# A graph network on one NeuronCore: long VectorE operations cut in pieces, other last groups, a shorter carry, a bias added by TensorE

## What is computed

```python
h = x @ W1 + b1
m = relu(concat([h[dst], h[src] - h[dst]]) @ W2 + b2)
m = relu(m @ W3 + b3)
x = layernorm(x + relu(segment_max(m, dst)))        # edge network

def gat(x, W, a_s, a_d, bias):                      # src, dst with loops added
    h = x @ W
    e = leaky_relu((h @ a_s)[src] + (h @ a_d)[dst])
    ex = exp(e - segment_max(e, dst)[dst])
    alpha = ex / segment_sum(ex, dst)[dst]
    return segment_sum(alpha[:, None] * h[src], dst) + bias

y = relu(gat(relu(gat(x, C1, ...)), C2, ...))
x = layernorm(x + y)
```

## Time and profile before

| | us |
|---|---|
| median of 3 runs | 5880.39 |
| lowest, highest | 5874.37, 5883.29 |
| the profiled execution's own time | 5872.45 |
| its span | 5871.2 |
| PE, DVE, ACT, POOL busy | 4931.6, 4098.0, 2658.7, 4399.4 |

### The profile page before, as it was taken

How to read it: one execution, slowest core, us unless ns; L and a number is a source line. 1 busy time by engine, 2 the same in 40 slices (tenths; PEclk the granted TensorE clock), 3 DMA queues, 4 the chain that set the end, 5 groups by cost and what they waited for, 6 DMA issues and landing times.

```text
span 5871.2 us, 119756 instructions
## 1 busy us (share of the span) xinstructions
PE 4931.6 (84%) x29429; PEld 3060.9 (52%) x29429; DVE 4098.0 (70%) x10676; ACT 2658.7 (45%) x8225; POOL 4399.4 (75%) x4585
## 2 busy tenths in 40 slices
PE   3688888888888729999999999943999999999991
PEld 2566666666666525555555555522555555555550
DVE  4344454444445448888888888864888888888886
ACT  2233333333333235555555555533555555555554
POOL 7777777777777677777777777767777777777775
PEclk6899999999999959999999999976999999999995
DMA  6677777777777724444444444432444444444442
GB/s 157 187 219 217 215 223 216 217 219 217 220 217 216 202 59 120 123 124 122 124 125 124 125 124 124 125 92 63 124 123 124 124 125 124 124 124 121 125 125 83
DMA packets 808269, 874.81 MB, mean 149 GB/s; under 512 B 133438, under 2 KB 635185, under 8 KB 807818
## 3 DMA queue, kind: packets, MB, share of 16 engines
q0 software_dynamic: 146016, 295.63, 19.7%
q1 hardware_dynamic: 390298, 361.70, 18.8%
q10 hardware_dynamic: 271504, 213.69, 13.9%
HBM read 536.74 MB, written 331.81 MB: 148 GB/s over the span
## 4 chain that ended last, share of the span: by engine, by line
POOL 51%; issue 21%; DVE 9%; PE 7%; DMA 6%; ACT 3%; DVEq 0%; POOLq 0%; SPq 0%; ACTq 0%
POOL ring_a L545 25%; POOL ring_a L485 22%; DMA ring_a<-H_table,src_i 6%; PE ps L1417 5%; DVE ring_b L1120 5%; ACT ring_a L746 2%; POOL ring_a L512 2%; POOL ad_edges L520 2%; POOL P_compact L498 1%; PE ps L1311 1%; DMA ring_a<-Q_table,src_i 1%; DVE ring_a L1074 1%; PE ps L1321 1%; DVE gz L1104 1%; DVE ring_b L1074 0%
## 5 line engine op out<-in xcount | busy, mean ns | idle before, releaser
L545 POOL DMA_INDIRECT ring_a<-H_table,src_i x2712 | 2588.2, 954 | 826.9 <-issue 755.9
L1417 PE MATMUL ps<-work,ring_a 128*128 128x390 bf16 x10752 | 1867.3, 330 | 238.5 <-DVE ring_a L1074 234.9
L485 POOL DMA_INDIRECT ring_a<-Q_table,src_i x1501 | 1432.8, 955 | 461.0 <-issue 453.0
L1417 PEld LDWEIGHTS ps<-work,ring_a 128*128 128x128 bf16 x10752 | 1015.8, 98 | 1065.2 <-DVE ring_a L1074 387.7
L1417 PE MATMUL ps<-work,ring_b 128*128 128x390 bf16 x8064 | 1407.7, 329 | 0.0
L638 ACT ACTIVATE code<-src_row,code_bias 128x128 int16<-128x128 int32 x2676 | 829.5, 389 | 1214.2 <-DVE ring_b L1074 1152.0
L1120 DVE SCALAR_TENSOR_TENSOR ring_b<-ring_b,gw,ring_a 128x129 f32<-128x129 f32 x3124 | 1092.0, 350 | 120.4 <-ACT ring_a L746 104.2
L948 DVE TENSOR_TENSOR_SCAN work<-ring_b,work,ps 128x512 f32<-128x512 bf16 x390 | 498.4, 1278 | 951.8 <-PE ps L1321 911.1
L1417 PEld LDWEIGHTS ps<-work,ring_b 128*128 128x128 bf16 x8064 | 787.0, 98 | 559.7
L746 ACT ACTIVATE ring_a<-ring_a,gw 128x129 f32<-128x129 f32 x3126 | 959.3, 390 | 0.0
L1074 DVE TENSOR_TENSOR ring_a<-code,ps 128x896 bf16<-128x896 int16 x1536 | 944.1, 615 | 1.2 <-issue 0.3
(11 more groups left out here) (267 smaller groups left out, 3625.2 us busy)
## 6 DMA issues: line engine op xcount, KB each, us to landing
run_sum<-ring_b SPq DMA_DIRECT2D x388, 520.0 KB
work<-P_compact SPq DMA_DIRECT2D x1563, 64.0 KB
ring_b<-rank_rows ACTq DMA_DIRECT2D x194, 512.0 KB, 5.2
run_max<-tab_flat ACTq DMA_DIRECT2D x194, 512.0 KB
one_rows<-H_table SPq DMA_DIRECT2D x3840, 0.5 KB
ring_a<-H_table,src_i POOLq DMA_INDIRECT x2712
src_row<-in_srcL SPq DMA_DIRECT2D x384, 64.0 KB, 3.0
ring_a<-Q_table,src_i POOLq DMA_INDIRECT x1501
```

The source lines that it names most:

```text
L485: pool.indirect_dma_start(out=q_ring[:, g % RING, j - j0, :], out_offset=None, in_=Q_table, in_offset=bass.IndirectOffsetOnAxis(ap=srcT_i[ ...
L545: pool.indirect_dma_start(out=h_ring[:, g % RING1, j - j0, :], out_offset=None, in_=H_table, in_offset=bass.IndirectOffsetOnAxis(ap=src_i[ ...
L1417: m = tensor.matmul(ps[parity][:, 0:3 * W], lhsT=hot_space[c // 4][:, c % 4, k - k0, :], rhs=split[:, k, :, :].rearrange("p s f -> p (s f) ...
```

## The change

- `short` cuts seven blocks in pieces of 3, 2 and 2. DVE operations over a batch (384, 256 and 256 elements in place of 896) are cut so: both in `count_rows`, the two subtractions of the Q split and of `project`, the residuals, and layer 0's bias. Operations over a whole row of 1562 to 1664 elements (`fresh`, the rank scan, `neg`) are cut in pieces of 384. L837, L847, L894 and the scan L1063 stay whole.
- `groups` ends 4, 4, 2, 1 in place of 4, 4, 3. `groups1` ends with one more full group and then 3, in place of 5, 5, 1, so that one more column in each layer is picked on PE and one gather fewer is issued on POOL (1355 in place of 1356).
- The chain for crossing runs clears its tiles before the wait, copies before it scans, clears one column of `state_shift` in place of the tile, waits for fewer of its own results, and reads one value straight from PSUM.
- The second layer's bias is added by PE to every row of H (the weights of a node's edges sum to one): for each block a product of a one-hot column with the bias row comes ahead of the product with C2. L1214 goes in layer 1.
- In the closing batches a batch is centred and normalised one batch later instead of two, and three blocks of each of the last two batches are normalised on DVE instead of ACT.

The diff at its core:

```diff
+def short(k0, k1):
+    cuts = [k0] + [k for k in range(k0 + 3, k1 - 1, 2)] + [k1]
+    return list(zip(cuts, cuts[1:]))
...
-    groups, groups1 = cut(L, G, 4), cut(L, G1, 5)
+    late_of = [0] * (B - 2) + [3, 3]
+    groups, groups1 = cut(L, G, 4), cut(L, G1, 3)
+    j0, j1 = groups.pop()
+    groups += [(j0, j1 - 1), (j1 - 1, j1)] if j1 - j0 > 1 else [(j0, j1)]
...
-            vector.tensor_tensor_scan(rank[:, :], ones[:, 0:1].to_broadcast([P, BL]), fresh[:, :], 0.0, ALU.mult, ALU.add).then_inc(dve.up(), 1)
-            vector.wait_ge(dve.sem, dve.n)
+            for a, e in spans:
+                vector.tensor_tensor_scan(rank[:, a:e], ones[:, 0:1].to_broadcast([P, e - a]), fresh[:, a:e],
+                                          rank[:, a - 1:a] if a else 0.0, ALU.mult, ALU.add).then_inc(dve.up(), 1)
+                vector.wait_ge(dve.sem, dve.n)
...
-                vector.tensor_tensor(split[:, at, 2, :], rest, split[:, at, 1, :], ALU.subtract).then_inc(split_low, 1)
+                for a, e in short(k0, k1):
+                    left = vector.tensor_tensor(split[:, a:e, 2, :], rest[:, a - k0:e - k0, :], split[:, a:e, 1, :], ALU.subtract)
+                left.then_inc(split_low, 1)
...
+                vector.memset(r["cc"][:, :], 0.0).then_inc(dve.up(), 1)
+                vector.memset(state_shift[:, :, 0:1], 0.0).then_inc(dve.up(), 1)
                 vector.wait_ge(last_spread, 3 * (layer + 1))
+                vector.tensor_copy(r["ma"][:, :], ps[5][:, 0:P]).then_inc(dve.up(), 1)
                 vector.tensor_tensor_scan(r["rs"][:, :], r["link"][:, :], ps[5][:, 0:P], -BIG, ALU.add, ALU.max).then_inc(dve.up(), 1)
...
-                vector.tensor_tensor(E1[:, at, 0:F], E1[:, at, 0:F],
-                                     bias[name][:, :].unsqueeze(1).to_broadcast([P, n, F]), ALU.add).then_inc(out_summed, 1)
+                if layer == 0:
+                    for a, e in short(k0, k1):
...
+                    if b >= 1:
+                        centre(*batches[b - 1], B + b - 1)
...
+                    def normalise_late(b):
+                        vector.wait_ge(centred, B + b + 1)
+                        for k in range(batches[b][1] - late_of[b], batches[b][1]):
+                            vector.tensor_scalar(x_sb[:, k, :], x_sb[:, k, :], s["rstd"][:, k:k + 1], s["centre"][:, k:k + 1],
+                                                 ALU.mult, ALU.add).then_inc(normed_late, 1)
...
-                        m = tensor.matmul(ps[2 + q % 2][:, i * W:(i + 1) * W], lhsT=turned1[:, (c0 + i) * P:(c0 + i + 1) * P],
-                                          rhs=conv_w[pc // B][:, :], start=True, stop=True)
+                        piece = ps[2 + q % 2][:, i * W:(i + 1) * W]
+                        if pc >= B:
+                            tensor.matmul(piece, lhsT=ident[:, 0:1].to_broadcast([P, P]), rhs=bias["c2"][:, :], start=True, stop=False)
+                        m = tensor.matmul(piece, lhsT=turned1[:, (c0 + i) * P:(c0 + i + 1) * P], rhs=conv_w[pc // B][:, :],
+                                          start=pc < B, stop=True)
```

More of the change, by code:

```diff
@@ L916, in vector_program @@
                         vector.wait_ge(q_low, n - 1)
-                    vector.tensor_tensor(q_rests[n % 2], q_stage[:, c * PIECE:(c + 1) * PIECE, :], q_split[c][:, :, 0, :],
-                                         ALU.subtract).then_inc(q_rest, 1)
+                    for a, e in short(0, PIECE):
+                        left = vector.tensor_tensor(q_rests[n % 2][:, a:e, :], q_stage[:, c * PIECE + a:c * PIECE + e, :],
+                                                    q_split[c][:, a:e, 0, :], ALU.subtract)
+                    left.then_inc(q_rest, 1)
                 if n >= 1:
@@ L921, in vector_program @@
                     vector.wait_ge(q_mid, n)
-                    vector.tensor_tensor(q_split[c][:, :, 2, :], q_rests[(n - 1) % 2], q_split[c][:, :, 1, :],
-                                         ALU.subtract).then_inc(q_low, 1)
+                    for a, e in short(0, PIECE):
+                        left = vector.tensor_tensor(q_split[c][:, a:e, 2, :], q_rests[(n - 1) % 2][:, a:e, :], q_split[c][:, a:e, 1, :],
+                                                    ALU.subtract)
+                    left.then_inc(q_low, 1)
             for layer in range(2):
@@ L1210, in vector_program @@
                                                     in1=tab[:, k, 0:F], op0=ALU.mult, op1=ALU.add).then_inc(dve.up(), 1)
-                    if layer == 1 and b >= 2:
-                        centre(*batches[b - 2], B + b - 2)
                     vector.wait_ge(dve.sem, dve.n)
-                    vector.tensor_tensor(E1[:, at, 0:F], E1[:, at, 0:F],
-                                         bias[name][:, :].unsqueeze(1).to_broadcast([P, n, F]), ALU.add).then_inc(out_summed, 1)
+                    if layer == 0:
+                        for a, e in short(k0, k1):
+                            left = vector.tensor_tensor(E1[:, a:e, 0:F], E1[:, a:e, 0:F],
+                                                        bias["c1"][:, :].unsqueeze(1).to_broadcast([P, e - a, F]), ALU.add)
+                        left.then_inc(out_summed, 1)
                     if layer == 0:
```

81 lines of the change are left out of this document (45 added, 36 removed).

## The result

The changed kernel takes 5841.47 us (median of 4 runs, 5838.68 to 5842.73) against 5878.10 for the kernel before (median of 4, 5874.37 to 5883.29): a ratio of 0.9939, 95% interval 0.9927 to 0.995. The profiled execution took 5841.24, its span is 5840.0; before 5872.45 and 5871.2.

A forecast was written before the change was run, and what follows sets the result against it. POOL, issuing one indirect DMA in about 1.25 us, was taken to bound the kernel. The terms summed to -26.0 from the profiled 5872.45, 5846.4; with that execution 7.9 below the median, the forecast was 5854.4, range 5843 to 5868.

The forecast's parts named there:

- bias on PE: Batches behind layer 0: POOL 8 us earlier by fewer stalls, columns 20.0 later by PE's products and the pieces: -5.0 us.
- The sum against the profiled execution: Terms sum to -26.0 from 5872.45, giving 5846.4; that execution is 7.9 below the median, so 5854.4.
- First projection: First projection's batches: 21 cut operations each save POOL 0.3 us of stall: -6.4 us.
- Opening: Opening: 0.7 us saved before Q's first gather, limited by the Q_table store, and 2.6 behind it: -3.3 us.
- `groups1`: End of each layer: one gather less on POOL and a shorter last group: -2.1 us a layer, -4.2 in all.
- `groups`: End of the edge network: the smaller last group doesn't help, since ranks are last instead of rows: +0.4 us.
- Crossing runs: DVE chain with POOL waiting at its end: fewer memsets, copies and waits save 0.9 us a layer, -1.8 in all.
- Closing batches: Closing stretch, bound by ACT: 1.0 us saved on the way to the last batch, 4.7 at its end.
- L1214's 1.1 on DVE is hidden behind ACT: Step in the closing batches: the 1.1 us of L1214 on DVE is hidden behind ACT.
- everything kept: Rival, chance 0.10: PE gets the upper clock early and the Q store isn't late, -33 us in all, 5848.
- PE stays at 1.2 GHz: Rival, chance 0.17: PE's clock stays low, the batches behind layer 0 gain nothing, -20.4 us, 5860.
- the pieces gain nothing: Rival, chance 0.10: cutting DVE's operations doesn't relieve POOL, by lock-step or the skill's rule, -11.3 us, 5869.

The follow-up runs named there:

- uncut kernel: The changed kernel with all DVE operations whole again, the three row-long ones in one piece each, all else kept: 5864.43 us.
- with the bias on DVE: The changed kernel with the second layer's bias added by DVE again, in pieces, and PE's 49 products with it gone: 5849.10 us.
- seven-piece kernel: The changed kernel with batch operations cut in seven pieces of one block instead of three, the row-long ones staying at 384: 5857.43 us.

## Why the prediction was wrong

Two steps of the sum failed: the last one, which added 7.9 us that belonged to one execution, and the term of the bias on PE, -5.0 where the stage gave -9.9.

- *The sum against the profiled execution.* Of the 12.9 us between forecast and result, 7.9 are the last step: "that execution is 7.9 below the median", carried over as if it belonged to the kernel. It belonged to one execution: the change's own profiled execution lies 0.2 from its median. Against the profile, the terms give -26.0 and the traces -31.2. That miss of 5.2 is nearly all the next term's.
- *The bias on PE* (-5.0, measured -9.9) was right in its mechanism and mis-sized in both of its parts. POOL's stalls were to give 8; they gave 10.6 (excess 13.0 before, 2.4 after; 13.9 in the uncut kernel). The excess before was read as 12.2, since the window of the earlier trace rows only touches its hundredth DMA and the sum counted it whole; and a stall behind pieces costs 0.11 an operation here (0.17 in the first projection), not 0.2. PE's products and the pieces were to make the columns 20.0 later; it was 14.3. Of that the products are 13.0, 1.9 a batch in place of 2.6, and the pieces the rest. The 2.6 doesn't follow from its own condition: a burst of 6.8 whose second half is at the upper clock lasts 3.4 + 1.7 = 5.1, 1.7 more than 3.4, which makes 7 x 1.7 + 1.8 = 13.7. (2.6 comes out if only half of the *added* 3.4 is faster.) Four of the seven bursts did better than that and three worse. The next transposes took 0.93 in place of 1.73, too, but they aren't on the chain: ACT takes them up only after the scaling, 8 us later. So 0.7 of the gain was eaten, not "about half": 128.41 with the products, 127.73 without.
- *First projection* (-6.4, measured -7.3): right in mechanism; 21 x 0.3 is 6.3, and the residual stall is again smaller than taken.
- *Opening* (-3.3, measured -3.75): near by luck. It was 0.7 ahead of Q's first gather and 2.6 behind it; it was 0.1 and 3.6. The rows ended 3.35 earlier, but the table's last store was issued 1.4 later than before (1.2 forecast), and POOL's gather came another 3.1 after that, so next to nothing of the rows counted. Behind it, the hindrance of the Q gathers and P scatters had been 5.75, not 4.0, since only the longest gather was counted, and fell to 2.1.
- *The rule of the Trainium skill* ("SBUF — State Buffer", Who interferes with whom), by which a tensor_tensor with two SBUF inputs would not hold descriptor generation: behind layer 0 the uncut and the cut kernel differ only in such operations, and in POOL's busy time by 109.2 against 97.7. For the indirect DMAs of this kernel the measurement decides against the inference. They take their node numbers from SBUF, and the same rule lets such an operation contend with what GpSimd reads; whether it is that reading which was held, no run tells. "VectorE: DVE Perf Modes" (The TRN2 errata), tiles of at least 512 elements: three pieces cost DVE 0.13 an operation, seven 0.39 (1.50 against 1.11), so the advice agrees with the rows, and seven lost. Three paid because DVE wasn't the bound.
- *Last groups.* `groups1` gave 1.75 a layer, 2.1 forecast. `groups` was to cost 0.4 and brought 0.4 in its own stretch (14.08 to 13.72), less than the 1.9 by which that stretch varies: the load was used 4.4 after its issue, with PE waiting 1.49, as forecast, but the last scan, turn and evacuation are shorter. The edge network as a whole came out 1.2 longer, and it moves by up to 2.7 between runs.
- *Crossing runs*: 0.95 a layer, 0.9 forecast.
- *Closing batches*: -6.0, -5.7 forecast, with cycle and end to 0.1. But the step "L1214's 1.1 on DVE is hidden behind ACT" is true of the old order only. In the new one it would cost 8.0, so PE's bias is what makes the order pay, and its net worth in this kernel is 7.3, not a loss of 3.
- *The rivals*: "everything kept" came nearest (-33 against the profile's -31.2), and by half of its reason: the products ate only 0.7 behind layer 0, but the store was late as forecast. "PE stays at 1.2 GHz" and "the pieces gain nothing" fell.

## What to carry to other kernels

Add the distance of one execution from its median to another kernel's forecast only after a second kernel shows it. Price two edits that meet on one cycle in a table of four, since a cost that one order hides the other may not: here each half alone gave nothing or a loss. And a cost hidden behind a bound engine is still there: 14.8 us of PE's products came to light as soon as POOL was no longer the bound, and there the pieces, which are worth 23 us where POOL is the bound (5864.43 against 5841.47), lost.

## What the runs showed of the hardware

- A run of short DVE operations without a gap can hold a POOL DMA as a whole: 4.07 beside twenty-one operations of 128 elements, where pieces of 384 and 256 at the same place let it through at 0.96. It need not: another such run in the same trace let one through at 0.94.
- A DVE tensor_tensor of 896 elements took 1.11 in one piece, 1.24 in three, 1.50 in seven.
- In six of seven bursts of 14 fp32 records (3.4 us) behind layer 0 the granted clock stayed at 0.50 or 0.51, before and with the bias on DVE. In the change's bursts of 28, each after 5.4 to 9.3 us of rest, it rose to 1.00 inside, at the middle or near the end, and they lasted 4.8 or 5.8; in the seven-piece kernel up to 6.4. The next transposes took 0.93 in place of 1.73. Products added to such a burst cost 0.25 each, near the 0.23 of the upper clock.
- On one chip the kernel before took 5880.01 and 7880.14 us on two occasions. In the second, DVE's and ACT's rows in the batches have the durations of the first; SP issued twelve single rows in 8.8 in place of 4.8, and PE was idle for 1082 us ahead of its edge products with nothing shown that it waited for.
